# Moving two steps in ScalarE's order in an attention and layer-norm kernel

## What is computed

```
x = x + layernorm(attention(layernorm(x)))
x = x + layernorm(ffn(layernorm(x)))
```

## Time and profile before

| | |
|---|---|
| median of 3 runs | 1924.92 us (1924.34 to 1929.66) |
| the profiled execution's own time | 1925.03 us |
| its span, first to last instruction | 1923.5 us |
| mean granted TensorE clock | 0.975 |
| busy, share of the span | TensorE 92%, VectorE 75%, ScalarE 44%, GpSimd 43% |
| DMA | 244.31 MB, mean 127 GB/s |

### The profile page before, as it was taken

The page is one execution under the profiler, slowest core; times in us unless marked ns, Lnnn a source line. Parts: engine busy times, 40 slices in busy tenths (PEclk is TensorE's granted clock), DMA queues, the critical chain, the costliest instruction groups (busy, mean ns, idle before and its releaser), DMA issues.

```text
span 1923.5 us, 55853 instructions
## 1 busy us (share of the span) xinstructions
PE 1760.5 (92%) x23040; PEld 1397.8 (73%) x23040; DVE 1437.2 (75%) x2824; ACT 838.0 (44%) x1800; POOL 831.4 (43%) x782
## 2 busy tenths in 40 slices
PE   5989999999999999989999999998999999999993
PEld 3777777777777777777777777777777777777772
DVE  6677777777777777867777777777777877768774
ACT  3344444444444444434444444444444444444443
POOL 1143444434434444434445345344445444344445
PEclk9999999999999999999999999999999999999996
DMA  5445555454555455545455544555555554544542
GB/s 197 106 111 132 139 118 131 115 140 122 125 135 127 117 141 129 123 122 143 111 131 123 133 123 122 137 127 122 138 131 133 127 133 119 139 122 119 135 117 66
DMA packets 361268, 244.31 MB, mean 127 GB/s; under 512 B 285876, under 2 KB 285876, under 8 KB 360503
## 3 DMA queue, kind: packets, MB, share of 16 engines
q1 hardware_dynamic: 361014, 240.75, 49.8%
HBM read 106.44 MB, written 67.11 MB: 90 GB/s over the span
## 4 chain that ended last, share of the span: by engine, by line
PE 29%; DVE 27%; POOL 15%; ACT 15%; issue 13%; SPq 0%; ACTq 0%; DMA 0%; POOLq 0%; DVEq 0%
PE ps_k L534 7%; PE ps_y L604 6%; PE ps_tv L534 6%; PE ps_q L534 5%; POOL probs L266 5%; POOL o_sb L288 5%; DVE probs L371 3%; DVE total L383 3%; DVE stC L415 3%; DVE stA L361 3%; ACT probs L486 3%; DVE top L369 3%; DVE stB L409 3%; ACT xT_hi L456 3%; PE ps_tv L527 2%
## 5 line engine op out<-in xcount | busy, mean ns | idle before, releaser
L266 POOL TENSOR_TENSOR probs<-probs,inv 128x512 f32<-128x512 f32 x128 | 136.1, 1064 | 557.4 <-DVE inv L389 557.4
L282 POOL TENSOR_TENSOR z<-z,b_row 128x512 f32<-128x512 f32 x128 | 192.2, 1521 | 142.7 <-DVE z L432 142.7
L329 DVE TENSOR_TENSOR xT_lo<-ps_tv,xT_hi 128x512 fp32r<-128x512 f32 x128 | 88.5, 691 | 172.2 <-ACT xT_hi L456 172.2
L288 POOL TENSOR_TENSOR o_sb<-o_sb,x 128x512 f32<-128x512 f32 x128 | 161.8, 1286 | 100.3 <-ACT o_sb L447 100.3
L534 PE MATMUL ps_k<-wk_hi,xT_hi 128*128 128x512 f32 x512 | 161.1, 437 | 19.7 <-issue 15.9
L486 ACT ACTIVATE probs<-probs 128x512 f32<-128x512 f32 x128 | 80.9, 632 | 223.9 <-DVE probs L371 223.9
L275 POOL TENSOR_TENSOR x<-x,res 128x512 f32<-128x512 f32 x128 | 162.9, 1294 | 1.7 <-ACT x L447 1.6
L396 DVE STREAM_TRANSPOSE kT<-ps_k 128x512 f32<-128x512 f32 x128 | 138.6, 1082 | 33.6 <-PE ps_k L534 33.1
L353 DVE TENSOR_TENSOR x<-ps_y,bo_row 128x512 f32<-128x512 f32 x128 | 88.1, 688 | 96.8 <-PE ps_y L604 94.5
L534 PE MATMUL ps_k<-wk_hi,xT_lo 128*128 128x512 f32 x512 | 150.0, 416 | 7.2 <-issue 7.2
L432 DVE TENSOR_TENSOR z<-z,g_row 128x512 f32<-128x512 f32 x128 | 88.6, 692 | 85.2 <-ACT z L447 84.4
(11 more groups left out here) (85 smaller groups left out, 3721.2 us busy)
## 6 DMA issues: line engine op xcount, KB each, us to landing
res<-in_xr SPq DMA_DIRECT2D x64, 512.0 KB, 4.4
k_bd<-kT SPq DMA_DIRECT2D x512, 64.0 KB, 2.0
v_d<-v_tok SPq DMA_DIRECT2D x128, 256.0 KB, 4.2
v_key<-v_d SPq DMA_DIRECT2D x128, 256.0 KB, 3.4
p_bd<-pT SPq DMA_DIRECT2D x512, 64.0 KB, 2.0
out<-o_sb SPq DMA_DIRECT2D x64, 512.0 KB, 4.9
x_in<-in_xa SPq DMA_DIRECT2D x63, 512.0 KB, 4.5
x<-in_wk SPq DMA_DIRECT2D x1, 1024.0 KB
```

Of the source, the lines that this page charges most:

```text
L266: nc.gpsimd.tensor_tensor(probs[t % 2][:, :, :, :].rearrange("p i u k -> p (i u) k"), probs[t % 2][:, :, :, :].rearrange("p i u k -> p (i ...
L282: nc.gpsimd.tensor_tensor(z[:, j, :], z[:, j, :], b_row[:, :], ALU.add).then_inc(z_done, 1)
L288: nc.gpsimd.tensor_tensor(o_sb[:, v % 2, j, :], o_sb[:, v % 2, j, :], x1[:, v % 3, j, :], ALU.add).then_inc(out_done, 1)
L329: nc.vector.tensor_tensor(xT_lo[t % 2][:, :, :], ps_tv[:, :].rearrange("p (c n) -> p c n", n=P), xT_hi[t % 2][:, :, :].bitcast(F32), ALU.s ...
```

## The change

ScalarE's order alone is changed. The copy of the values out of `ps_tv` moves from behind norms B and C to ahead of them (it stays behind A), and the shift of norm X moves from the end of an even slot to the odd slot behind it, between the exponential and `normalise`. For s odd, (s + 3) // 2 is the same pair as (s + 4) // 2 was in the slot before.

```
                     nc.scalar.activation(probs[...], probs[...], ACT.Exp, scale=SCALE).then_inc(exp_done, 1)
+                v = (s + 3) // 2
+                if s % 2 == 1 and 1 <= v < NV:
+                    shift("X", v)
                 t = s + 2
                 if 2 <= t < NT:
                     normalise(t)
...
                         scaled(x1[:, v % 3, j, :], x1[:, v % 3, j, :], "A", v, j).then_inc(lny_done, 1)
+                t = s
+                if tile(t):
+                    act.wait_ge(v_ready, t + 1)
+                    if t >= 2:
+                        act.wait_ge(v_stored[t % 2], DMA * (t // 2))
+                    nc.scalar.activation(v_tok[t % 2][:, :], ps_tv[:, :], ACT.Copy).then_inc(vtok_done, 1)
                 v = (s - 5) // 2
                 if s % 2 == 1 and pair(v):
                     shift("B", v)
...
                         scaled(o_sb[:, v % 2, j, :], z[:, j, :], "C", v, j).then_inc(lnz_done, 1)
-                t = s
-                if tile(t):
-                    act.wait_ge(v_ready, t + 1)
-                    if t >= 2:
-                        act.wait_ge(v_stored[t % 2], DMA * (t // 2))
-                    nc.scalar.activation(v_tok[t % 2][:, :], ps_tv[:, :], ACT.Copy).then_inc(vtok_done, 1)
-                v = (s + 4) // 2
-                if s % 2 == 0 and 1 <= v < NV:
-                    shift("X", v)
```

## The result

| | before | after |
|---|---|---|
| median (4 runs each) | 1925.21 us | 1791.84 us (1791.19 to 1793.92) |
| ratio | | 0.9305, interval 0.9288 to 0.9321 |
| span of the profiled execution | 1923.5 us | 1790.9 us |
| mean granted TensorE clock | 0.975 | 0.989 |
| TensorE busy | 92% | 96% |

The change takes 133.4 us off; 76.2 were forecast, and the range had its lower end at 1843. The direction and the new pace were right; a second gain of 57 us was not seen at all.

What follows compares the result with a forecast made beforehand. ScalarE's order was taken to bound the kernel, TensorE waiting for v_tok: 58.0 + 15.8 + 5.3 = 79.1, less 2.9 for short stalls, gives 76.2 off 1925.0, so 1849 us; range 1843 to 1872.

Steps and rivals of the forecast that it cites:

- What bounds the kernel: A ring through ScalarE's order makes TensorE wait for v_tok: a pair takes 28.33, a slot without waits 13.31.
- The parts of the change: Times from slot start for moved shift X, v_tok, B, C and SP's queue; tightest slack 0.6, p_bd before ps_o.
- The 16 long slots stay: TensorE slots of 15.18 to 19.80 keep their stalls of 1.5 to 4.0 us; no v_tok wait left to remove.
- I take 0 and keep 15.6: Bound on TensorE's stalls lengthening once v_tok waits go: 15.6 us more at worst, 0 taken in the sum.
- the 2.9 charged for short stalls: Four slots' short TensorE stalls, hidden in v_tok waits, would show and take 2.9 us from the gain.
- the census: Count of TensorE's 124 slots by length; those under 15 us give 79.1 us over 13.31.
- Growth of the stalls: Rival: TensorE's stalls grow by the waits they lose, up to 15.6 us, 1849 to 1864; chance 0.11.
- A new ring between 13.31 and 13.66: Rival: p_bd's landing or qT holds even slots, costing 12 to 37 us, 1861 to 1886; chance 0.13.
- No change: Rival: the gap before the transposes is owed to one bank serving transposes and values; 1925; chance 0.06.
- slower: Rival: shift X still waits, holding normalise, with v_tok added on ScalarE's ring; 60 us more, 1985; chance 0.04.

Runs made afterwards that it cites:

- e9: Kernel before with only shift X moved, plus 19 idle TensorE instructions a slot so blocks end away from slots' starts: 1796.9 us (0.9340).
- e11: Kernel before with only v_tok moved, 19 idle TensorE instructions a slot and 128 more ahead of the loop, swapping block ends between even and odd slots: 1870.2 us (0.9730).
- e2: Kernel before with only v_tok moved ahead of B and C, shift X left in place, no idle instructions: 1935.6 us (1.0067).
- e10: Kernel before with only v_tok moved, plus 19 idle TensorE instructions a slot, blocks ending at 72 in even and 200 in odd slots: 2055.7 us (1.0683).
- e5: Changed kernel with 19 idle TensorE instructions a slot, so blocks end 72 and 200 instructions behind slots' starts: 1780.3 us (0.9240).
- e3: Kernel before with 19 idle TensorE instructions a slot, so blocks end 72 and 200 instructions behind slots' starts: 1879.3 us (0.9759).
- e4: Kernel before with 19 idle TensorE instructions a slot and 62 more ahead of the loop; blocks end 10 behind even slots' starts: 2107.0 us (1.0946).
- e7: Changed kernel, 19 idle instructions a slot, block ends apart, plus a wait before the transposes on TensorE's own previous output projection: 1820.1 us (0.9441).

## Why the prediction was right and wrong

**What bounds the kernel: right.** 13.31 was the floor, and both kinds of slot fell to it.

**The parts of the change: right, to a few hundredths.** From the odd slot above: `xT_lo` at +1.26 (said +1.30), `rsX` done at +2.74 (+2.7), `shX` without a wait at +4.66 (about +4.5), v_tok at +10.71 (+10.75), B's products from +11.95 (+11.96), the products with g at +12.79 (+12.8), then `x<-ps_y` at +0.80 and `xT_lo` at +1.40 of the even slot (+0.8, +1.42).

**The step that failed: "The 16 long slots stay".** It was put into the sum as a constant, with the reason that no wait for v_tok is left in these slots to remove, and the bound beside it allowed only for growth: "I take 0 and keep 15.6". The runs showed the other sign. Of the 73.0 us that these slots had over 13.31, 17.7 at most are left, which gives 55 us, and the 2.9 charged for short stalls weren't due: 76.2 + 2.9 + 55.3 = 134.4, what the 124 slots gave. The rows that could have told were in the timelines. The bound compared a slot with a named wait of 1.04 (921.96) with one that has no named wait (1024.28). But TensorE waited for v_tok in both; ScalarE's rows are

```profile
921.24 0.57 ACT L513 ACTIVATE v_tok<-ps_tv 128x512 f32<-128x512 f32 x1
...
1023.56 0.58 ACT L513 ACTIVATE v_tok<-ps_tv 128x512 f32<-128x512 f32 x1
```

and v_tok ends at 921.81 and at 1024.14, 0.15 and 0.14 before the transposes. So it is in all 16 long slots (0.14 or 0.15). The stalls end 4.8 to 6.4 us after the slot's start whatever the named wait. I read it as "the wait doesn't help the fetch". What the experiments showed is that the fetch is asked for only when the wait is over, so that releasing TensorE earlier brings it forward. A stall whose cause wasn't known was also bounded on one side only.

**How the gain splits.** With the ends apart the stalls are out of both kernels, and the two edits give 1879.3 - 1780.3 = 99.0 by semaphores alone. The stalls cost the kernel before 1925.2 - 1879.3 = 45.9 and the changed one 11.5, a difference of 34.4; together 133.4. The 76.2 of the forecast is smaller than 99.0 because a stall hid the v_tok wait at the end of its slot: without the stalls the kernel before has 105.2 over 13.31 in its slots, where the census had 79.1. Shift X alone gives 82.4 of the 99.0 (e9); v_tok alone 9.1, or 16.7 with its later loop start (56.67 for 49.06) taken off (e11).

**The rivals.** Growth of the stalls (0.11): wrong in sign. A new ring between 13.31 and 13.66 (0.13): the place was right, waits before `ps_o`, but they are small, some 15 us in all in the 124 slots, and about ten of these are owed to the fetch and not to p_bd by itself (5.2 us of such waits are left in e5). No change and slower: not seen, but e2 shows how near they lay: v_tok moved without the shift left the time within 0.7%, through waits for p_bd, a way that I hadn't listed. That a block's packet has a part in e2's long slots is carried over from e10 and e11; in e2 itself the last p_bd before an even slot took over 2.5 us to land in 26 of 60.

**What stays open.** Which packets share an engine's queue in which order wasn't tried apart; that the place of the block's end delays p_bd is shown by the swap, how 1.5 to 2 us come out of a packet of 1.2 us is only read from one slot. Nor was it measured how far ahead the sequencer can run, or what sets the time from its release to the packet: in the changed kernel packets start 1.1 to 2.7 behind v_tok's end in most cases, and in the others 3 to 6.

## What to carry to other kernels

A wait right ahead of a short burst of many instructions can cost more than its idle time: in this kernel it also kept the sequencer from asking for the next block of instructions. So look at where stalls without a releaser stand in the engine's own count of instructions. If they stand at one position modulo 256, there are two ways: free the wait in front of the burst early (2.0 us did here, 0.5 didn't), or move the blocks' ends by idle instructions (19 a slot took 46 us from the kernel before, and 11.5 from the changed one). A block's end can do harm in a second way too, when its packet runs beside a transfer that is just due (e10). And a stall without a known cause has a bound on both sides.

## What the hardware showed that was not expected

- 62 idle instructions ahead of a loop changed the time by 228 us (e3 and e4), and 128 of them by 185 us (e10 and e11), with nothing else changed.
- One instruction packet of 16 KB took 0.9 to 1.5 us (the kernel before). With such a packet at +1.6 of the even slots the last transfer of p_bd landed after 3.7 us in place of 2.0 (e10 and e11).
- A wait in TensorE's stream on TensorE's own last matmul cost 0.34 to 0.39 us a slot (e7).
- After the stall of 3.81 us in e4 the next projection ran at the lower granted clock (0.50 over 1107.93 to 1109.70); the mean clock was 0.922 in e4 with its 61 long slots and 0.988 in e5 with none.
